# Adding x ahead of the base part in the second pass of a one-core conditioned LoRA layer

## The reference

```python
y     = einsum('bct,bcd->bdt', x, cond_w[cond])         # 64x64 matrix per entry
base  = einsum('bsi,oi->bso', y, W_org)                 # 1024 x 1024
q     = einsum('bi,ki->bk', y.mean(axis=1), Wq)
coef  = softmax(q @ lora_keys.T / sqrt(128))            # over 8 experts
h     = einsum('bsi,eir->bser', y, lora_down)
delta = einsum('be,bser,ero->bso', coef, h, lora_up)
out   = x + base + delta
```

## Time and profile before

| | us |
|---|---|
| median of 3 runs | 775.73 |
| the profiled execution, whole | 774.48 |
| span from its first to its last instruction | 772.6 |
| PE / DVE / ACT / POOL busy | 715.3 / 488.5 / 237.4 / 167.3 |
| mean granted TensorE clock (1 is 2.4 GHz) | 0.982 |

### The profile page before, as it was taken

One profiled execution on the slowest core, in us unless ns is written; L12 is line 12 of the kernel. 1 busy time (PEld: TensorE's weight loads), 2 busy tenths in 40 slices (PEclk: granted clock), 3 DMA queues, 4 the chain that ended last, 5 costly groups with the idle time before them and its releaser, 6 DMA issues.

```text
span 772.6 us, 10492 instructions
## 1 busy us (share of the span) xinstructions
PE 715.3 (93%) x3385; PEld 595.6 (77%) x3385; DVE 488.5 (63%) x757; ACT 237.4 (31%) x456; POOL 167.3 (22%) x141
## 2 busy tenths in 40 slices
PE   4697999999999999999997739999999999999997
PEld 4585887888878878788786627888888888888885
DVE  3569539356383573744825497777777777777773
ACT  4345326134162342523513542222222222222220
POOL 2530203002021030110300002333333333333332
PEclk9899999999999999999999978999999999999999
DMA  9952343442633524435321434666666666666643
GB/s 265 321 168 75 123 139 131 140 135 96 169 111 116 170 104 132 132 126 138 121 76 61 163 118 150 220 221 224 223 217 226 213 230 219 220 223 226 221 165 106
DMA packets 83672, 128.10 MB, mean 166 GB/s; under 512 B 18458, under 2 KB 51234, under 8 KB 81570
## 3 DMA queue, kind: packets, MB, share of 16 engines
q1 hardware_dynamic: 75024, 125.26, 50.0%
q10 hardware_dynamic: 8594, 2.17, 1.4%
HBM read 77.07 MB, written 50.33 MB: 165 GB/s over the span
## 4 chain that ended last, share of the span: by engine, by line
PE 78%; DVE 11%; issue 6%; ACT 1%; DMA 1%; POOL 1%; ACTq 1%; DVEq 0%; POOLq 0%; SPq 0%
PE x_ps L1285 21%; PE h_ps L1201 21%; PE w_ps L1285 15%; PE w_ps L1224 7%; PE y_ps L1179 6%; PE x_ps L1224 6%; DVE gs L763 1%; DVE tb_l L760 1%; DVE ga_l L760 1%; PE y_ps L1274 1%; DVE ysum L773 1%; DVE org_f L760 1%; DVE blk L763 1%; DVE yg L791 1%; DVE up_raw L760 1%
## 5 line engine op out<-in xcount | busy, mean ns | idle before, releaser
L459 POOL TENSOR_TENSOR blk<-blk,blkx 128x512 f32<-128x512 f32 x64 | 97.9, 1530 | 288.4 <-DMA blkx<-in_x_dram 159.4
L1285 PE MATMUL x_ps<-tb_h,ba_h 128*128 128x512 f32 x256 | 100.7, 393 | 15.1 <-DVE blk L763 14.1
L763 DVE TENSOR_TENSOR blk<-w_ps,blk 128x512 f32<-128x512 f32 x96 | 65.9, 687 | 60.7 <-PE w_ps L1285 31.6
L1201 PE MATMUL h_ps<-yq_h,down_h 128*128 128x512 f32 x256 | 101.8, 398 | 0.9 <-ACT ones_r L499 0.9
L1285 PE MATMUL x_ps<-tb_h,ba_l 128*128 128x512 f32 x256 | 100.1, 391 | 0.0
L1285 PE MATMUL x_ps<-tb_l,ba_h 128*128 128x512 f32 x256 | 100.1, 391 | 0.0
L1201 PE MATMUL h_ps<-yq_h,down_l 128*128 128x512 f32 x256 | 99.7, 390 | 0.0
L1201 PE MATMUL h_ps<-yq_l,down_h 128*128 128x512 f32 x256 | 99.7, 390 | 0.0
L843 DVE TENSOR_TENSOR g<-h_ps,coef 128x512 f32<-128x512 f32 x32 | 22.1, 691 | 117.7 <-PE h_ps L1201 98.2
L433 POOL TENSOR_TENSOR yq_l<-y_full,yq_h 128x512 fp32r<-128x512 f32 x32 | 46.4, 1451 | 198.6 <-ACT yq_h L499 198.6
L499 ACT ACTIVATE y_full<-y_ps 128x512 f32<-128x512 f32 x58 | 34.6, 596 | 163.9 <-PE y_ps L1179 163.9
(11 more groups left out here) (91 smaller groups left out, 1242.4 us busy)
## 6 DMA issues: line engine op xcount, KB each, us to landing
x_sb<-in_x_dram SPq DMA_DIRECT2D x32, 512.0 KB, 4.1
y_dram<-y_full SPq DMA_DIRECT2D x64, 256.0 KB, 2.7
r_dram<-blk SPq DMA_DIRECT2D x64, 256.0 KB, 2.4
yb<-y_dram SPq DMA_DIRECT2D x32, 512.0 KB, 7.6
blk<-r_dram SPq DMA_DIRECT2D x16, 1024.0 KB, 6.8
blkx<-in_x_dram SPq DMA_DIRECT2D x32, 512.0 KB, 6.9
out_dram<-blk SPq DMA_DIRECT2D x64, 256.0 KB, 3.9
x_sb<-in_L_ffn_W_org_dram SPq DMA_DIRECT2D x8, 512.0 KB, 3.6
```

The lines of the kernel that those rows point to most:

```text
L459: pool.tensor_tensor(blk[p % 3][:, b, :], blk[p % 3][:, b, :], blkx[:, h, n, :], ALU.add).then_inc(x_added, 1)
L763: nc.vector.tensor_tensor(dst, a, b, ALU.add).then_inc(done, 1)
L1201: mm = nc.tensor.matmul(h_ps[:, m % 2, :], down[w][:, k, m * P:(m + 1) * P], yq[s][:, k, :], start=(k == 0 and i == 0), stop=(k == KC - 1 ...
L1285: mm = nc.tensor.matmul(bank, ba[s][n][:, k, :], tb[w][n][:, k, :], start=(first and k == 0 and i == 0), stop=(k == 3 and i == 2), skip_gr ...
```

## The change

The addition of x moves: POOL adds it to the lora part as soon as both are loaded, and DVE's `take_b` waits for that (`x_added`) where it waited for the load of the lora part. A store waits for DVE's last addition into its block. The x loads of pair p + 2 are issued with those of the lora part and of y; from pair 1 on each waits until the blocks of the pair before have had their x from `blkx`. In pair 15, PE's order becomes P6, P2, P5, P7, P3, P4.

```diff
             def load_xb(p, h):
+                if p >= 1:
+                    sp.wait_ge(x_added, 4 * p - 2 * (1 - h))
                 sp.dma_start(blkx[:, h, :, :]..., x_rows[p, h]).then_inc(xb_loaded[h], 16)
-            def store_out(p, b, added):
-                sp.wait_ge(x_added, 4 * p + added)
+            def store_out(p, b, ready):
+                sp.wait_ge(ready, p + 1)
...
             load_xb(0, 0)
             load_xb(0, 1)
+            load_xb(1, 0)
+            load_xb(1, 1)
             for p in range(NP):
-                store_out(p, 0, 1)
-                store_out(p, 3, 2)
+                store_out(p, 0, o11_ready)
+                store_out(p, 3, o22_ready)
...
                     load_yb(p + 2)
-                store_out(p, 1, 3)
-                if p + 1 < NP:
-                    load_xb(p + 1, 0)
-                store_out(p, 2, 4)
-                if p + 1 < NP:
-                    load_xb(p + 1, 1)
+                    load_xb(p + 2, 0)
+                    load_xb(p + 2, 1)
+                store_out(p, 1, o12_ready)
+                store_out(p, 2, o21_ready)
...
-            def add_x(p, b, ready):
+            def add_x(p, b):
                 h, n = b // 2, b % 2
-                pool.wait_ge(ready, p + 1)
+                pool.wait_ge(r_loaded[p % 3], 16 * (p // 3 + 1))
                 pool.wait_ge(xb_loaded[h], 16 * (p + 1))
...
             for p in range(NP):
-                add_x(p, 0, o11_ready)
-                add_x(p, 3, o22_ready)
-                add_x(p, 1, o12_ready)
-                add_x(p, 2, o21_ready)
+                for b in range(4):
+                    add_x(p, b)
...
             def take_b(p, b, after, ready):
                 dve.wait_ge(base_done[after], p + 1)
-                dve.wait_ge(r_loaded[p % 3], 16 * (p // 3 + 1))
+                dve.wait_ge(x_added, 4 * p + b + 1)
...
             for p in range(NP):
-                base_2(p)
-                base_6(p)
-                base_7(p)
-                base_5(p)
                 if p + 1 < NP:
+                    base_2(p)
+                    base_6(p)
+                    base_7(p)
+                    base_5(p)
                     base_1(p + 1)
+                else:
+                    base_6(p)
+                    base_2(p)
+                    base_5(p)
+                    base_7(p)
                 base_3(p)
                 base_4(p)
```

## The result

The changed kernel takes 783.89 us (median of 4 runs, 782.61 to 784.28) against 775.90 for the kernel before (4 runs, 775.24 to 776.19): 1.0103, 95% interval 1.0089 to 1.0117, so 8.0 us slower where 8.0 were forecast. Timed once more in a later session it was 782.69 against 775.30, 1.0094 (1.0079 to 1.0110).

What follows compares the result with a forecast made beforehand. The prediction took TensorE, 93% busy and without waits in the middle of the pass, as the bound. Its terms, 5.42 + 1.8 + 0 + 2.14 - 1.34 = 8.0, on 775.73 gave 783.7 us, range 781.0 to 787.0.

Steps and rivals of the forecast that it cites:

- Start of pair 0: Start of the second pass: take_b of block 0 waits for x's load and addition, delaying PE by 5.42 us.
- The additions in a row: Pair 0: four to six GpSimd additions hold up DVE, so take_b of block 2 comes late for P5, +1.8 us.
- The low clock: PE's restart in pair 0: P6's slow steps taken as unchanged, 0 us, between 1 less and 1 more.
- Rival 1: Pair 0: the additions in a row cost nothing, 781.9 us in all; chance 0.17.
- Pairs 1 to 14: Middle pairs: additions follow the load one pair ahead and hide; 0 us, 19.04 a pair.
- Rival 2: Pairs 1 to 14: y load comes late with 1 MB of x behind it, 13 us, 797 in all; chance 0.06.
- Rival 3: All later pairs: re-timed traffic shortens PE's 0.2267 us step, giving 766.8 or 769.8 us; chance 0.02.
- Rival 4: Pair 0: x's load and addition stay hidden, leaving pair 15's +0.8, 776.5 us in all; chance 0.02.
- Pair 15: Last pair: PE waits 1.54 us ahead of P6 and P5, saves 0.94 ahead of P3; +2.14 us.
- Behind PE: End of the kernel: GpSimd's last addition goes, so the last store is issued earlier, -1.34 us.
- inner range: Whole kernel: the forecast's own range, 782.3 to 785.4 us.
- outer range: Whole kernel: range reaching over rival 1 and the upper bounds of pairs 0 and 15, 781.0 to 787.0 us.

Runs made afterwards that it cites:

- e1: Kernel before, with DVE's take_b of block 0 of pair 0 also waiting for the first x load; 779.37 us against 775.23, 1.0056.
- e4: Changed kernel, but block 0 of pair 0 gets x after the base part, second x half loaded first; 776.41 us against 775.23 for the kernel before.
- e8: Changed kernel, with POOL holding pair 1's additions until o22_ready of pair 0; 782.78 us against 775.42 for the kernel before, 1.0098.
- e9: Changed kernel, POOL adding to blocks 0 and 2 of pair 0, the rest only after b2_ready; 782.21 us against 775.42 for the kernel before.
- e5: e4 with PE's old order in pair 15; 774.32 us against 775.30 for the kernel before, 0.9983.
- e2: Kernel before, with only PE's order in pair 15 changed to P6, P2, P5, P7, P3, P4; 777.67 us against 775.23, 1.0033.
- e7: Kernel before with PE's new order in pair 15 and DVE's order made for it, nothing else; 773.82 us against 775.30, 0.9983.

## Why the prediction was right

- **Start of pair 0, +5.42.** Measured +5.71 and +5.53 in two profiles. e1 has the load's part by itself (+4.07), and e4 takes the whole away. The load took 4.2 from its issue to the addition in the first of the two, 3.9 before; addition and hand-over took 1.37 (470.81 to 472.18) where 1.33 were worked out.
- **The additions in a row, +1.8.** This is the term with the largest error. The mechanism held, the size did not: P5 began 8.26 after the restart in both profiles of the changed kernel, against 7.01 before, +1.25. (The prediction's 7.17 is 0.16 too high: the chain's 4.45 for P6 reaches to 469.90, P7 started at 469.74.) My walk put take_b of block 2 at the end 8.93 after the restart; it was 8.21 (481.13 less 472.92). No step was wrong in kind; five of them, the four held-up ones and take_b, each came out 0.1 to 0.2 shorter, so the split ended 5.91 after the restart instead of 6.38.
- **The low clock, 0.** P6's twelve steps took 5.13 and 4.90 in the two profiles, against 4.29 before, which the prediction had left unchanged. So PE was done with P7 at 7.88 and 7.65, and the gap ahead of P5 was 0.38 and 0.60, where the prediction named 1.8 as a sign. The two delays run side by side: e8 without the last held-up instruction begins P5 at 7.56, so 0.7 of the 1.25 go with DVE and about 0.55 stay with the slow steps of that execution. Rival 1 (the additions in a row cost nothing) is out by the profiles of e8 and e9, narrowly: the difference is 0.6 to 0.7 us at P5, which the times of the whole kernel can't tell.
- **Pairs 1 to 14, 0.** 19.04 a pair from P5 of pair 1 on, and e5's 301.77 against 301.71. Rival 2 (the y load late) is out: y lands 6.4 to 8.9 after issue with 1 MB of x right behind it, not later than before. The prediction left open which half of what the Trainium skill says ("DMA: Bandwidth & Descriptors", section "Queues, rings and completion order") would count here, descriptors consumed in ring order or completion that isn't first in, first out: no price of the second half shows in this trace.
- **Rival 3 (PE's step).** The step stayed 0.2267 with all additions moved; whatever sets it here, it is not their place. Rival 4 (the waits don't bind) fell with e1.
- **Pair 15, +2.14.** Measured: two gaps of 1.86 and 1.77 for one of 1.17, less one step, +2.23, and 0.14 more in the slower steps behind the additional wait; e2 has +2.4 in time. Both chains were the ones priced: end_o21 and the low part of P6, which is the first DVE instruction behind it and not the second as the prediction words it, and end_o11 with take_b of block 2. The chain ahead of P6 is 0.1 longer than the one ahead of P5, so 1.54 was a little low for it.
- **Behind PE, -1.34.** Measured -1.34; e5 gets it alone.

The errors, +0.3, -0.55, +0.2, cancel, so the agreement of the total to 0.2 us is partly luck. In its parts the prediction is right within 0.6. Its inner range, 782.3 to 785.4, isn't added up from its terms: with the low clock left at nothing, their lower bounds together give 780.2, which also lies below the outer range, and their upper ones 786.5.

## What to carry to other kernels

Moving an addition from behind a product to ahead of it moves its input's load to the head of the first turn too; where that turn already waits for the buffer's release, the load and the addition come on the path once, and that can outweigh what the last turn saves. Exempt the first turn's first block (e5) and keep the rest. An order of TensorE's products only pays with the order of the queue that releases them: the same PE order was a loss of 2.4 us with DVE's old order (e2) and a gain with the new (e7).

## What the runs showed of the hardware

The low clock behind PE's idle time (granted clock 0.56 and 0.50 in the windows shown, the 1.2 GHz level) did not last the same in every execution. Counted in steps of 0.40 us or more from the restart on, where a full-speed step is 0.23, it was 6, 6, 7, 9, 10 and 10 steps in the six profiles with 13.7 between PE's starts, and 9, 10, 10, 10, 11 and 13 in the six with 17.8 to 19.4. The longer idle seems to go with more slow steps, but the two sets overlap, and what decides is open.

A VectorE instruction of 128x512 with two SBUF inputs takes 0.68 us by itself. Where it met a GpSimd addition it took up to 1.78 us in the rows shown and 1.84 at most in the twelve profiles. In the row of additions above the two engines took turns: four additions in 5.87 us, with VectorE's instructions at 1.06, 1.77 and, for the split of 2.28, 2.77 beside them. One that reads PSUM stayed at 0.69 (472.18, 475.46, 480.45 above) right among them, and never took more in the second pass of any of the twelve profiles.
